# One fused stage per layer in a spectral tower, with batch statistics taken from the mixed spectra

## The reference, cut to what matters

```python
h = x @ fc0_w + fc0_b                       # x: (64, 64, 64, 3)
for l in range(4):
    xf = rfft2(h)                           # 32 x 16 modes are kept
    sc = irfft2(modewise_mix(xf, w1[l], w2[l]))   # 64x64 complex mix at each mode
    pw = einsum('bihw,oi->bohw', h, pw_w[l]) + pw_b[l]
    y = sc + pw
    y = (y - mean(y)) * rsqrt(var(y) + eps) * gamma[l] + beta[l]   # over batch and pixels
    h = gelu(y)
out = gelu(h @ fc1_w + fc1_b) @ fc2_w + fc2_b
```

## Time and profile before

| | us |
|---|---|
| median of 3 runs | 4404.04 (4381.96 to 4449.41) |
| span of the profiled execution | 4441.0 |
| PE busy | 3288.5 (74%) |
| DVE busy | 2394.9 (54%) |
| ACT busy | 2086.9 (47%) |
| data moved | 1120.67 MB, mean 252 GB/s |
| mean granted TensorE clock | 0.868 |

### The profile page before, as it was taken

One profiled execution on the slowest core, in us unless ns is written; L12 is line 12 of the kernel. 1 busy time (PEld: TensorE's weight loads), 2 busy tenths in 40 slices (PEclk: granted clock), 3 DMA queues, 4 the chain that ended last, 5 costly groups with the idle time before them and its releaser, 6 DMA issues. The chain is left out here.

```text
span 4441.0 us, 122046 instructions
## 1 busy us (share of the span) xinstructions
PE 3288.5 (74%) x54724; PEld 2081.7 (47%) x54724; DVE 2394.9 (54%) x3232; ACT 2086.9 (47%) x1724; POOL 28.9 (1%) x48
## 2 busy tenths in 40 slices
PE   6878866666888565596886556768877998559777
PEld 4756644455555343473554334745542222543432
DVE  3466668753666587544665777346651000554556
ACT  2133354421666644214665543236667998222321
POOL 0000000000000000000000000000000000100000
PEclk8989988888999888898998778989998999669688
DMA  8978887678999867598999676889996542003053
GB/s 305 351 192 241 238 265 271 256 288 336 345 391 380 295 249 264 228 327 330 381 377 333 248 264 249 321 294 399 391 340 231 190 173 99 10 10 68 1 97 67
DMA packets 181646, 1120.67 MB, mean 252 GB/s; under 512 B 25497, under 2 KB 31841, under 8 KB 107262
## 3 DMA queue, kind: packets, MB, share of 16 engines
q1 hardware_dynamic: 140924, 843.27, 52.7%
q10 hardware_dynamic: 39234, 269.45, 17.5%
q0 software_dynamic: 1024, 1.05, 0.1%
HBM read 708.56 MB, written 405.14 MB: 251 GB/s over the span
## 5 line engine op out<-in xcount | busy, mean ns | idle before, releaser
L602 PEld LDWEIGHTS bank<-fb,arena 64*64 64x64 f32 x16384 | 671.9, 199 | 512.9 <-issue 498.8
L602 PE MATMUL bank<-fb,arena 64*64 64x128 f32 x16384 | 677.9, 293 | 236.8 <-ACT arena L659 183.2
L659 ACT ACTIVATE arena<-bank,pwb 128x1024 f32<-128x1024 f32 x512 | 558.7, 1111 | 472.5 <-PE bank L593 337.0
L703 DVE BATCH_NORM_STATS2 stats<-arena 128x6 f32<-128x512 f32 x1024 | 627.8, 676 | 176.4 <-ACT arena L659 175.9
L843 ACT ACTIVATE arena<-arena,shift,scale 128x1024 f32<-128x1024 f32 x384 | 443.5, 1229 | 438.4 <-DMA arena<-y_dram 437.9
L593 PE MATMUL bank<-arena,wst 64*64 64x512 f32 x4096 | 629.9, 633 | 11.0 <-issue 10.9
L695 DVE STREAM_TRANSPOSE arena<-bank 128x512 f32<-128x512 f32 x512 | 321.1, 685 | 501.5 <-PE bank L579 501.5
L803 PE MATMUL bank<-arena,fwq 32*32 32x512 f32 x6144 | 322.6, 824 | 362.4 <-DVE arena L848 319.3
L651 ACT ACTIVATE arena<-arena,shift,scale 128x2048 f32<-128x2048 f32 x192 | 401.4, 2092 | 353.4 <-issue 206.2
L444 PE MATMUL bank<-arena 64*64 64x128 f32 x8192 | 455.4, 393 | 108.0 <-ACT arena L459 89.0
L444 PEld LDWEIGHTS bank<-arena 64*64 64x64 f32 x8192 | 395.0, 153 | 168.1 <-issue 118.8
(11 more groups left out here) (195 smaller groups left out, 2364.4 us busy)
## 6 DMA issues: line engine op xcount, KB each, us to landing
arena<-y_dram SPq DMA_DIRECT2D x224, 2048.0 KB, 10.2
y_dram<-arena ACTq DMA_DIRECT2D x256, 1024.0 KB, 13.2
arena<-in_w_modes SPq DMA_DIRECT2D x32, 2048.0 KB, 17.2
arena<-spec_in SPq DMA_DIRECT2D x32, 2048.0 KB, 14.7
spec_out<-arena SPq DMA_DIRECT2D x128, 512.0 KB, 15.6
arena<-spec_out SPq DMA_DIRECT2D x112, 512.0 KB, 16.9
spec_in<-arena SPq DMA_DIRECT2D x24, 2048.0 KB, 13.6
spec_in<-arena SPq DMA_DIRECT2D x4, 4096.0 KB, 12.0
```

The source lines that it names most:

```text
L602: mm = pe.matmul(hpx(bank[4 + T % 2 * 2 + i][CHAN[v], :])[:, :, j * S:(j + 1) * S], a2[p % 2][CHAN[i], v, :, 4 * T + j], hpx(fb2[CHAN[i], :]),
L659: act.activation(hpx(yout[u])[:, :, T * BK:(T + 1) * BK], banks[:, 4 + T % 2 * 2:6 + T % 2 * 2, :], ACT.Identity, bias=pwb[:]).then_inc(y_ ...
L703: dve.bn_stats(stats[:, p * 48 + 6 * t:p * 48 + 6 * t + 6], hpx(yout[p % 2])[:, i, T * BK:(T + 1) * BK]).then_inc(y_seen, 1)
```

## The change

It rebuilds the tower around one stage per layer.

- **Statistics.** The mean and variance of y are worked out in the mix stage from the mixed spectra (Parseval), so they are ready before the inverse. For this PE also multiplies the incoming spectra by the pointwise weights (`product`), ACT copies that out of PSUM and sums squares, and DVE sums cross products. The weights of chunk 0 need an even part (`w_even`), which POOL makes in spectrum0 for layer 0 and in the first fused stage for the others. Layer 0 takes the pointwise energy from a Gram matrix of x.
- **Fused stage** (`fuse`, layers 0 to 2) in place of inverse and forward. Per pair: rows, turn, spectral; the stored pointwise part is added by a multiply with the identity (in layer 0 with `wx` on x itself); ACT writes gelu(scale*y+shift) from PSUM to SBUF; PE computes the next layer's pointwise part (`next_of`), ACT copies it over h (`evict`) and sums its squares; DVE and PE run the forward transform of h. 2 MB are loaded and 2 MB stored per pair, in runs of 16 KB.
- **Last stage** (`last`) in place of inverse 3 and head: DVE adds the stored part to PSUM's spectral part, then gelu, fc1, gelu, fc2.
- `rows` now writes half the channels at a time for both parts, transposed within the bank: the row index is stride 1 and the channel stride 32 in PSUM. The DVE turns then go 1024 elements at a time.

Between mix and fuse the barriers drop from three per layer to two. The tail is the same but for addresses. The core of the diff:

```diff
@@ spectrum0 @@
+            load_modes(sp, 0, 0)
+            load_weights(sp, 0, 1)
+            sp.wait_ge(even_stored, 64)
+            load_even(sp, 0)
             for t in range(NB):
                 sp.wait_ge(fc0_first, 4 * t + 4)
...
+            for i in range(4 * NQ):
+                for wh in range(2):
+                    x = x0_all[:, i, wh * 96:(wh + 1) * 96]
+                    mm = pe.matmul(bank[2][0:96, 0:96], x, x, start=(i == 0 and wh == 0), stop=(i == 4 * NQ - 1 and wh == 1))
@@ mix @@
+            def product(n):
+                c, v = n // 2, n % 2
...
+                if n > 1:
+                    pe.wait_ge(mixed_turned, (l * NU + n - 1) * 2)
...
+                z = both(c)
+                for q in range(4):
+                    for h in range(2):
+                        m0 = v * K1 + h * M1 + 4 * q
+                        if q % 2 == 0:
+                            mm = pe.matmul(bank[4 * v + q][ROW[h], :], wst[ROW[0], :],
+                                           z[ROW[0], :, :, m0:m0 + 4].rearrange("p r b m -> p m r b"),
+                                           start=True, stop=True, tile_position=(0, h * C))
+                        else:
+                            o = bank[4 * v + q][ROW[h], :].rearrange("p (k r b) -> p k r b", k=4, r=2)
+                            for r in range(2):
+                                mm = pe.matmul(o[:, :, r, :], (wst, wneg)[r][ROW[1], :],
...
+            def spectra(n):
...
+                pe.wait_ge(prod_copied, l * NU + n + 1)
...
+            product(0)
+            for n in range(NU):
+                spectra(n)
+                if n + 1 < NU:
+                    product(n + 1)
...
+            def copy_product(n):
+                act.wait_ge(prod_done, l * NU + n + 1)
...
+            for n in range(NU):
+                square(n)
+                if n + 1 < NU:
+                    copy_product(n + 1)
+                if n % 2 == 0 and n // 2 + 1 < NCH:
+                    rotate(n // 2 + 1)
@@ rows, in fuse and last @@
+            for r in range(2):
+                for v in range(2):
+                    for par in range(2):
+                        mm = pe.matmul(bank[2 * s + v][CHAN[par], :].rearrange("p (c r k) -> p r k c", c=16, r=2)[:, r],
+                                       ga[k_p, r * S:(r + 1) * S], grp[p // Q % 2][k_p, :, par * Q + q, hc * 16:(hc + 1) * 16],
@@ fuse @@
+        ROWS_SLOT = (0, 1)
+        Y_SLOT = (0, 0, 1, 0)
+        NEXT_SLOT = (0, 1, 1, 1)
...
+                if T == 1:
+                    pe.wait_ge(h_made, n * 4 + 1)
+                if T == 2 and p > 0:
+                    pe.wait_ge(squared, n * 4)
+                if T == 3:
+                    pe.wait_ge(squared, n * 4 + 1)
+                spectral(pe, p, T, Y_SLOT[T], False)
+                for i in range(2):
+                    for v in range(2):
+                        mm = pe.matmul(bank[2 * Y_SLOT[T] + i][CHAN[v], :], add_w[i], pb[p % NS][CHAN[i], v, T * BK:(T + 1) * BK],
...
+            def gelu(p, T):
+                act.wait_ge(y_done, n * 4 + T + 1)
+                act.activation(chunk(p, T), slot(Y_SLOT[T]), ACT.Gelu, bias=shift[:], scale=scale[:]).then_inc(h_made, 1)
+            def evict(p, T):
...
+                act.activation(chunk(p, T), slot(NEXT_SLOT[T]), ACT.Copy).then_inc(evicted, 1)
+                act.activation(slot(NEXT_SLOT[T]), slot(NEXT_SLOT[T]), ACT.Square, accum_out=acc[:, p * 4 + T:p * 4 + T + 1]).then_inc(squared, 1)
@@ last @@
+            for n in range(NP + 1):
...
+                if now:
+                    y_of(n, 2)
+                    first(4 * n, 0)
+                    first(4 * n, 1)
+                if after:
+                    rows_of(n + 1, 1)
+                if before:
+                    second(4 * n - 1)
+                if now:
+                    first(4 * n + 1, 0)
+                    y_of(n, 3)
```

More of the change, by code:

```diff
@@ new lines, in turn @@
+            def turn(n):
+                c, v = n // 2, n % 2
+                if v == 0 and c > 1:
+                    dve.wait_ge(mixed_stored[c % 2], l * (NCH * 32) + (c // 2 * 64))
+                    dve.sem_inc(waited[dve.engine], 1)
+                modes = banks[:, 4 * v:4 * v + 4, :].rearrange("p q (k r b) -> p b r (q k)", k=4, r=2)
+                for j in range(2):
+                    dve.transpose(m_sb[c % 2][:, 4 * j:4 * j + 4, v, :], modes[:, 32 * j:32 * j + 32]).then_inc(mixed_turned, 1)
@@ new lines, in vector_mix @@
+            rotate(0)
+            for n in range(NU):
+                cross(n)
+                turn(n)
+                if n % 2 == 0 and n // 2 + 1 < NCH:
+                    rotate(n // 2 + 1)
+            base = l * BN_STEPS
+            dve.wait_ge(layer_loaded, l * 96 + 96)
+            dve.wait_ge(crossed, (l * NU + NU) * 2)
+            dve.sem_inc(waited[dve.engine], 1)
+            dve.tensor_tensor(acc_p[:], acc[:], acc_w[:], ALU.mult).then_inc(bn_step, 1)
+            dve.scalar_tensor_tensor(out=bn[:, 9:10], in0=dc[:, 1:2], scalar=0.5, in1=dc[:, 0:1], op0=ALU.mult, op1=ALU.add).then_inc(bn_step, 1)
@@ L909, in tensor_head @@
[L909 to L919 removed]
+        FC_SLOT = (2, 1)
@@ new lines, in sync_last, with load @@
+        def sync_last(sp):
+            l = L - 1
+            def load(p):
+                if p >= NS:
+                    sp.wait_ge(fc1_done, (p - NS + 1) * 8)
+                load_pair(sp, p, True)
+            load_group(sp, l, 0, slice(NCH - 1, NCH))
+            load(2)
+            load(3)
+            for n in range(NP):
+                load_piece(sp, l, n)
+                if n > 1 and n + 2 < NP:
+                    load(n + 2)
+                if n == 6:
+                    sync_load_weights(sp)
@@ L1426, in build @@
         x63 = at(W, NT); W += NT
-        assert W <= HO + 2 * BK
-        combB = [at(upper + i * 8 * BK, 8, BK) for i in range(2)]
+        assert W <= lower and lower + 16 * BK <= HO + 2 * BK
+        combB = [at(lower + i * 8 * BK, 8, BK) for i in range(2)]
         comb_dram = [nc.dram_tensor(f"comb{m}", [(E0, E1)[m], TG * BK], F32, kind="Internal").ap() for m in range(2)]
```

1164 lines of the change are left out of this document (676 added, 488 removed).

## The result

The changed kernel takes 5886.06 us (median of 4 runs, 5868.47 to 5894.93), the kernel before 4415.83 (median of 4, 4381.96 to 4449.41). The ratio is 1.337, with a 95% interval of 1.329 to 1.346: slower by a third. I had forecast 4312 and a range up to 4550.

The account below looks back on a forecast made before the run. No single engine was taken to bound the tower, so fusing would overlap engines and move less data. Terms +33 +408 -40 -267 -227 = -93 on 4404 gave 4312 us; 8-in-10 range 4190 to 4550.

Parts of the forecast that it names:

- The last stage: Stage replacing inverse 3 and head: 17.6 us per pair from PE and ACT, 597 us against 824, -227.
- The fused stages: Layers 0 to 2: 650 us per stage against 706, 754 and 757 before, -267 together.
- the clock and the gaps: Fused stage: clock 0.97 since PE's gaps are under 0.6 us; half clock 3% of the time, 12 us more.
- no longer binds: Fused stage: DMA's 168 MB take 460 us at 364 GB/s, so DMA does not bind the stage.
- the loop itself: Fused stage: longest loop 19.4 us per pair; times 32 plus first and last pair, 638 us.
- my rival of the loosely running loop: Fused stages: one more us of hand-overs per pair and a clock of 0.9, 3 times 45, 4447 us; 14%.
- The mix: Mix stages: 13.5 us per half, 226 us per layer against about 124, +408 over four layers.
- the slow rate of the product: Mix: product runs at L444's slower rate, 3.5 us plus 0.4 for tile conflicts, 3.9 us per half.
- Mix to first rows: Step from mix to the first rows: 13 us against 14.9 in layer 0 and 25.8 in the others, -40.
- The opening: Before the first mix: first spectrum stores wait for POOL's rounds, starting near 68 instead of 37.8; +33 us (20 to 60).
- The strided PSUM write: Rival on rows: writing PSUM at stride 32 halves the rate, 0.86 to 1.72 us, total 4519 us; 20%.
- The product on two tiles: Rival in mix: product takes 7 us, 276 us per mix, 4 times 50 more, total 4512 us; 9%.

Follow-up runs that it names:

- last_four: Changed kernel with the last stage's plane load written as four transfers of 64 partitions in place of two: 5166.2 us, ratio 1.168.
- no_planes: last_four with loads and stores of the planes left out in the fused stages of layers 1 and 2: 4723.87 us.
- no_stats: paced without products, their copies, PE's wait for them and the crossings in the mix of layers 1 to 3: 4495.17 us.
- rows_flat: paced with rows writing its 256 columns to PSUM next to each other in place of 32 elements apart: 4701.23 us.
- paced: last_four with planes stored and loaded in quarters of 0.5 MB spread over the pair, same bytes: 4704.58 us, ratio 1.062.

## Why the prediction was wrong

**The last stage (-227 forecast, +487 measured; -184 with the one edit).** The step that failed is one that I didn't make: this transfer stands at nothing in the sum. I worked out PE's and ACT's time per pair and no DMA's: the text says nothing of how the planes reach the last stage, though the diff shows that this load has a pattern of its own. 2.5 MB per pair at the 364 GB/s of the earlier trace rows are 7 us, and I would have found it hidden. The kernel before reads its planes with 128 partitions in front; here the first dimension is 2. In last_four a pair takes 19.3 us (599.7 over 31 pairs) where I had 17.6, and the stage 640 where I had 597: that part was sized 7% low.

**The fused stages (-267 forecast, +519 measured).** Two steps failed.

The first is the clock and the gaps: "For the clock I take the 0.97 of the mix stretch, since PE's gaps in this loop are under 0.6 us". I counted only the gaps that waits make. The stands on the instruction queue, 132 to 147 us per stage in layers 1 and 2, and the half clock that comes with them (201 us of this stage in last_four, 22 in no_planes) make up the 218 to 224 us between 936 or 942 and the 718 without planes. The sentence that DMA "no longer binds" was right for bytes (share 0.62) and false for the time: its bursts held up another queue. The kernel before had the same thing in small. In layer 1 its trace has 14 such stands within groups, 32 us, 12 of them in the forward stage, so it was there to be read, in the waits that end with "issue" inside a running group. The change made it worse on both sides: the forward transform's 512 columns per matmul became 256, the rows' too, so the stage fetches 123 packets in place of 78, while 4 MB go back to back behind one wait.

The second is the loop itself: 19.4 us per pair forecast, 21.1 at best and 21.7 on average in no_planes, which is 718 in place of 650. The timeline of no_planes shows where. PE through two thirds of a pair, from h_dft (L973) on:

```profile
1825.63 2.76 PE L973 MATMUL bank<-arena,ghq 32*32 32x256 f32 x128
1828.32 1.19 PE L814 MATMUL bank<-fb,arena 64*64 64x128 f32 x32
1829.34 1.03 PE L922 MATMUL bank<-arena,ident 64*64 64x512 f32 x8
1830.19 1.03 PE L942 MATMUL bank<-arena,wst 64*64 64x512 f32 x8
1831.88 1.21 PE L814 MATMUL bank<-fb,arena 64*64 64x128 f32 x32 [0.66 <-ACT arena L1012]
...
1835.43 1.09 PE L804 MATMUL bank<-arena,ga 64*64 64x256 f32 x16 [0.57 <-ACT arena L1012]
1836.46 1.50 PE L956 MATMUL bank<-arena,fwq 32*32 32x256 f32 x64
1837.88 1.29 PE L814 MATMUL bank<-fb,arena 64*64 64x128 f32 x30
```

ACT's gelu, and its square with the sum:

```profile
1806.92 1.20 ACT L1012 ACTIVATE arena<-bank,shift,scale 128x1024 f32<-128x1024 f32 x1 [2.40 <-PE bank L922]
1803.39 1.02 ACT L1020 ACTIVATE bank<-bank 128x1024 f32<-128x1024 f32 x1
1804.33 0.19 ACT L1020 ACTIVATION_READ_ACCUMULATOR bank<-bank 128x1 f32 x1
```

From start to start h_dft takes 2.69 where I had 2.5, the spectral part of y 1.02 for 0.91, rows 1.03 for 0.86, w_dft (L956, the first half of the forward transform) 1.42 for 1.3. Each short matmul costs a little more than its columns; over all of PE's list that is 18.5 us per pair in place of 17.3.

The loop that holds the undisturbed pairs at 21.1 is also not quite the one that I followed. The square with its sum isn't on it: that ends 0.6 us before the y that needs its slot, and copy, square and sum take 2.03 together where I had 2.3. It runs through y, gelu, y, gelu, rows, w_dft, y, gelu, rows, w_dft, y, next, h_dft. At my prices that sum is 19.0 as well, so the number was right by luck as far as the path goes. Measured it is 2.1 more. The three pieces of y, hand-over, gelu and hand-over take 3.57 each for 3.19: the y 0.11, the gelu 0.14 (its own 1.20 counts, since PE waits for its end, not the 1.06 from one start to the next), the hand-overs 0.13. That makes 1.1, and the rest is rows twice (0.3), w_dft twice (0.25), h_dft (0.2), and the last y and next (0.2). Small "issue" gaps of 0.66 to 0.78 us, which remain even here, lift the mean from 21.1 to 21.7. The term mis-sized is thus the loop, 638 us of the stage's 650. This is my rival of the loosely running loop, and at 718, with nearly the full clock, it was larger than the 695 that I gave it with a clock of 0.9.

**The mix (+408 forecast, +362 measured).** Right in mechanism and nearly in size: 12.81 per half against 13.5, with 7.03 for 7.3, 3.70 for 3.9, and 2.08 for the drain, the copy and the semaphore, which I had at 2.3. Right too was the slow rate of the product: its four steps of 0.86 us, at full clock, hold the columns of 4 records of 512 each, half the rate of the dense rows.

**Mix to first rows (-40 forecast).** Right in three layers (14.6, 15.4, 15.3 for 13), and no_stats brought the 25 us back as this explanation demands. In the last layer the same two-engine loads stood in the way: 82, and 22 without them.

**The opening (+33 forecast, +39.5 measured).** Within its bounds of 20 to 60. The trace shows the wait that I had put there: SP's even weights go at 75.4 and the first stores at 75.9, where I had 68 and the kernel before 37.8. POOL's rounds came 11.7 us apart where I had 9. No experiment was made on it.

**The rivals.** The strided PSUM write is refuted by rows_flat. The Trainium skill, page "PSUM — Partial Sum Buffer", section Specifications (TRN2), has it that any non-contiguous pattern slows matmuls significantly; 1.02 us with and without the stride says that this one does not. The prediction could have known more: it says that every PE write in the rows of before is contiguous, but L602 writes two runs of 64 elements apart from each other (64x2x64 in the order of PE's list) and takes 0.91 us where the dense rows take 0.86. The product on two tiles would have shown halves of 16.6. None of the rivals had a DMA on few engines or a late instruction fetch in it, so the range had no place for either.

**What the change could have brought.** With the one fault mended and most of the other (paced), the kernel stands at 4702 against 4441 in the profiled runs. The last stage gives 184. The three fused stages cost 29, 25 and 5 more than what they replace, because the loop of 21.7 us per pair is not faster than inverse and forward one after the other. The opening costs 40 and the four mixes 362. Even with the statistics of three layers left out it takes 4495, at a ratio of 1.014 (1.006 to 1.022). The trade itself is a loss: 91 us per layer for statistics that only the last stage pays back, by two times that. None of the measured versions beats the kernel before. Whether a kernel with only the last layer fused would do so wasn't tried: its statistics need the pointwise part of every plane of layer 2 computed, squared and stored first, by the rows above about 3.4 us of PE and 8 of ACT per pair in the stage ahead (an estimate).

## What to carry to other kernels

Read every transfer of a change on its own, the moved and reshaped ones above all: bytes over bandwidth was its time here when its access pattern began with 64, and not when it began with 2. When PE stops in the middle of a group whose waits are over, look at the instruction queue, and then at what fills the DMA engines just before: many short matmuls and transfers bunched behind one wait made each other worse, and spreading the same bytes over the loop gave back 462 us here. A stage that fuses two should be costed at start-to-start times of its own short instructions, not at those of the long ones that it replaces.

## What the runs showed of the hardware

- A DMA whose pattern begins with a dimension of 2 had two packets under way and moved 52 GB/s, and what stood behind it in the same queue waited with it (45.4 us to land, 11.2 in the same stage with 64 in front).
- PE's instructions came in packets of 16 KB, about 250 records each. Under long stretches of data about one per stretch came late, and PE stood for up to 7 us, some 140 us per stage. Runs of 16, 4 or 2 KB made no difference to that; fewer bytes at a stretch did. The Trainium skill, page "Runtime: NRT & Kernel Launch", section Instruction fetch mechanics, calls the cost of crossing a 16 KB boundary mostly hidden. That is so without the planes (1.4 to 5 us of stands in a stage) and not beside them.
- The granted clock fell with these stands: 0.89 in the fused stages with them, 0.98 without.
- Matmuls of 256 columns written to PSUM 32 elements apart took as long as those written side by side, 1.02 us per 16 records.
- The mode products of mix took 0.22 us per four records at a granted clock of 0.60 (1299.7 to 1306.1 of the changed kernel) and of 1.00 (1063.8 to 1072 of the kernel before) alike.
